# Routing weights spread over partitions by DMAs and multiplied in by GpSimd, in place of TensorE's spreading products

## The reference

```python
xV = einsum('btd,kdr->btkr', Q_side, V)          # r = 64 per expert
cum_yW = cumsum(einsum('btd,kdr->btkr', K_side, W), axis=1)
weights = softmax(gelu(Q_side @ w1.T + b1) @ w2.T + b2 + expert_bias)
out = einsum('btkr,kdr->btd', xV * cum_yW * weights[..., None], U)
out = (out + weights @ b) / n_valid              # n_valid: 1, 2, 3, ...
```

## Time and profile before

| what | value |
|---|---|
| median of 3 runs | 1653.61 us (1653.0 to 1655.18) |
| profiled execution | 1654.62 us, span 1652.9 us |
| mean granted TensorE clock | 0.996 |
| busy: PE / DVE / ACT / POOL | 1563.5 / 937.7 / 684.4 / 284.2 us |
| DMA | 116.48 MB, 38.5% of 16 engines' span |

### The profile page before, as it was taken

How to read it: one execution, slowest core, us unless ns; L and a number is a source line. 1 busy time by engine, 2 the same in 40 slices (tenths; PEclk the granted TensorE clock), 3 DMA queues, 4 the chain that set the end, 5 groups by cost and what they waited for, 6 DMA issues and landing times.

```text
span 1652.9 us, 36914 instructions
## 1 busy us (share of the span) xinstructions
PE 1563.5 (95%) x15489; PEld 1112.8 (67%) x15489; DVE 937.7 (57%) x2048; ACT 684.4 (41%) x1224; POOL 284.2 (17%) x346
## 2 busy tenths in 40 slices
PE   5899999999999999999999999999999999999997
PEld 4576675767757676676757767576675767667674
DVE  6665672737537484564837567274763748447461
ACT  3426245261543517243362523626254351634425
POOL 2011121211112111121201212021111201112111
PEclk9999999999999999999999999999999999999999
DMA  8514417072350906218071350806326080530800
GB/s 207 63 31 88 80 34 123 10 117 51 76 89 4 151 15 104 61 38 130 4 122 45 77 91 21 125 21 106 62 64 100 4 139 27 96 69 23 132 4 14
DMA packets 128186, 116.48 MB, mean 70 GB/s; under 512 B 19251, under 2 KB 127668, under 8 KB 127972
## 3 DMA queue, kind: packets, MB, share of 16 engines
q1 hardware_dynamic: 128020, 114.12, 38.5%
HBM read 73.43 MB, written 34.34 MB: 65 GB/s over the span
## 4 chain that ended last, share of the span: by engine, by line
PE 76%; DVE 14%; ACT 5%; issue 4%; POOL 1%; DMA 0%; DVEq 0%; ACTq 0%; POOLq 0%
PE PS L587 33%; PE PS L714 8%; DVE block_peak L1204 4%; PE PS L793 3%; PE PS L825 3%; PE PS L732 3%; PE PS L856 3%; PE PS L766 3%; PE PS L807 3%; PE PS L772 3%; DVE prod L1273 2%; PE PS L726 2%; DVE prod L1276 2%; ACT HE L1029 2%; PE PS L746 2%
## 5 line engine op out<-in xcount | busy, mean ns | idle before, releaser
L1446 POOL TENSOR_TENSOR PL<-prod,PH 128x512 fp32r<-128x512 f32 x128 | 164.5, 1285 | 792.7 <-ACT PH L1003 792.7
L1003 ACT ACTIVATE PH<-prod 128x512 fp32r<-128x512 f32 x128 | 80.8, 631 | 428.8 <-DVE prod L1276 428.8
L587 PE MATMUL PS<-XH,WH 128*128 128x512 f32 x512 | 220.4, 430 | 4.5 <-DVE XL L1145 1.9
L587 PE MATMUL PS<-XH,WL 128*128 128x512 f32 x512 | 203.6, 398 | 0.0
L587 PE MATMUL PS<-XL,WH 128*128 128x512 f32 x512 | 203.2, 397 | 0.0
L1204 DVE TENSOR_REDUCE block_peak<-PS 128x4 f32<-128x512 f32 x288 | 186.9, 684 | 4.2 <-PE PS L746 4.2
L993 ACT ACTIVATE prod<-PS 128x512 f32<-128x512 f32 x128 | 76.3, 596 | 231.3 <-PE PS L587 220.3
L1029 ACT ACTIVATE HE<-PS 128x512 f32<-128x512 f32 (+1 forms) x320 | 159.7, 552 | 26.1 <-PE PS L807 23.5
L1197 DVE TENSOR_REDUCE peak<-PS 128x4 f32<-128x512 f32 x192 | 125.6, 685 | 41.0 <-PE PS L732 41.0
L1273 DVE TENSOR_TENSOR prod<-PS,prod 128x512 f32<-128x512 f32 x128 | 88.1, 689 | 104.6 <-PE PS L701 104.6
L714 PE MATMUL PS<-UH,PH 128*128 128x256 f32 x512 | 139.5, 306 | 0.0
(11 more groups left out here) (195 smaller groups left out, 3154.8 us busy)
## 6 DMA issues: line engine op xcount, KB each, us to landing
parts_d<-area SPq DMA_DIRECT2D x32, 768.0 KB, 5.1
area<-parts_d SPq DMA_DIRECT2D x128, 192.0 KB, 12.4
area<-parts_d SPq DMA_DIRECT2D x32, 576.0 KB, 12.5
tok<-in_L_attn_x_dram SPq DMA_DIRECT2D x16, 512.0 KB, 6.5
xt<-in_L_attn_x_dram SPq DMA_DIRECT2D x16, 512.0 KB, 3.9
out_dram<-xt SPq DMA_DIRECT2D x16, 512.0 KB, 3.7
area<-parts_d SPq DMA_DIRECT2D x96, 64.0 KB, 5.9
Vs<-Va SPq DMA_DIRECT2D x24, 204.0 KB, 7.6
```

The costliest lines, as they stand in the source:

```text
L587: ins = e.matmul(ps, a, b, start=first and k == 0, stop=last and k == n - 1, skip_group_check=True)
L1003: e.activation(PH[:, h, :], prod[:, j % 3, :], ACT.Copy).then_inc(phi)
L1446: e.tensor_tensor(PL[:, j % 2, :], prod[:, j % 3, :], PH[:, j % 2, :].bitcast(F32), ALU.subtract).then_inc(plo)
```

## The change

TensorE's `product` matmul, the matrix `spread` with its memset and its three selects, bank 4's use by `product` and the semaphore `w_ps` are removed. In `gate_parts` VectorE also turns the float32 gates (in 32x32 blocks) into `weights_t`; SP writes that to DRAM (`weights_d`) in four DMAs, waits for them, and for each block j reads two rows of it back, each repeated over 64 partitions, into one of three 128x512 buffers `wide` (two of them are `rest`). GpSimd multiplies `prod` by it in place, in the new stage `weigh`, which stands in the list right behind the x stage of the block. VectorE's `product` keeps the multiplication by bank 3 only and waits for `weigh`. Blocks 0 to 2 are read back in the stage `gate_parts` itself; block j + 3 after block j's `weigh`. ScalarE's copy to `WT` no longer waits for `w_ps`, and the running sum of the next chunk waits for the last `weigh` stages, since it overwrites `rest`.

```diff
@@ the list of stages
-                order.append([(add_x, ch, j + 1, part) for part in range(2)])
+                order.append([(add_x, ch, j + 1, part) for part in range(2)] + [(add_weigh, ch, j + 1)])
...
     def add_product(ch, j):
-        add("product", ch, j, uses=["bank4"])
+        add("product", ch, j)
+
+    def add_weigh(ch, j):
+        add("weigh", ch, j)
+        if j + WIDE < 2 * KB:
+            add_wide(ch, j + WIDE)
+
+    def add_wide(ch, j):
+        add("wide", ch, j, uses=[f"wide{j % WIDE}"])
+
+    def add_gate_parts(ch):
+        add("gate_parts", ch)
+        for j in range(WIDE):
+            add_wide(ch, j)
...
         add_cout(ch, 0)
         if nxt:
+            add_weigh(ch + 1, 0)
             run([(add_x, ch + 1, 1, part) for part in range(2)])
+            add_weigh(ch + 1, 1)
         for k in range(DB):
             add_on("cparts", ch, k, uses=[score_use()])
         if nxt:
             run([(add_x, ch + 1, 2, part) for part in range(2)])
+            add_weigh(ch + 1, 2)
         add_finish(ch)
@@ buffers
-        spread = sb("spread", [KSTK, 2 * KB, P], BF16)
+        weights_t = sb("weights_t", [P, T * 32])
+        wide = [rest[:, 0, :], rest[:, 1, :], sb("wide2", [P, C])[:, :]]
+        weights_d = nc.dram_tensor("weights_d", (2 * KE, C), F32, kind="Internal").ap()
@@ TensorE
-                elif kind == "product":
-                    ch, j = key
-                    q.wait_ge(bank_read[7], use("bank7", "weight_rows", ch))
-                    take(4, *stage)
-                    e.matmul(psum(4), spread[:, j, :], WT[:, :], start=True, stop=True).then_inc(w_ps)
@@ VectorE, turn
+                        q.wait_ge(weighed, nth("weigh", ch - 1, 6 + k))
@@ VectorE, gate_parts
+                    q.wait_ge(weights_out, 16 * 4 * ch)
+                    e.transpose(weights_t[:, :].rearrange("p (t w k) -> p t w k", t=T, w=2),
+                                gate[:, 2:4].rearrange("p w t k -> p t w k")).then_inc(weights_turned)
+                    q.wait_ge(weights_turned, ch + 1)
@@ VectorE, product
-                    q.wait_ge(bank_read[2], use("bank2", "x", ch, j, 0))
-                    q.wait_ge(w_ps, nth(*stage))
-                    e.tensor_tensor(prod[:, r, :], psum(4), prod[:, r, :], ALU.mult).then_inc(bank_read[4])
-                    q.wait_ge(bank_read[4], use("bank4", *stage))
+                    q.wait_ge(weighed, nth("weigh", ch, j))
                     q.wait_ge(c_ps, nth(*stage))
                     e.tensor_tensor(prod[:, r, :], psum(3), prod[:, r, :], ALU.mult).then_inc(bank_read[3])
@@ GpSimd
-                    for n, first in enumerate((0, 3 * HD, 5 * HD)):
-                        view = spread[:, :, :].rearrange("r j (a m) -> r (j a) m", a=2)
-                        select(view, [[-1, 4 * KB], [0, R]], -first, 1, ALU.not_equal, 1.0, after=8 + n if n else 0)
...
+                elif kind == "weigh":
+                    ch, j = key
+                    q.wait_ge(bank_read[2], use("bank2", "x", ch, j, 0))
+                    q.wait_ge(wide_in[j % WIDE], 16 * use(f"wide{j % WIDE}", "wide", ch, j))
+                    e.tensor_tensor(prod[:, j % 3, :], prod[:, j % 3, :], wide[j % WIDE], ALU.mult).then_inc(weighed)
@@ SP
+                elif kind == "gate_parts":
+                    ch, = key
+                    q.wait_ge(weights_turned, ch + 1)
+                    for i in range(WIDE):
+                        q.wait_ge(wide_in[i], 16 * (use(f"wide{i}", "wide", ch, i) - 1))
+                    for g in range(4):
+                        e.dma_start(weights_d.rearrange("k (t g r) -> g k t r", t=T, g=4)[g],
+                                    weights_t[32 * g:32 * g + 2 * KE, :].rearrange("k (t r) -> k t r", t=T)).then_inc(weights_out, 16)
+                elif kind == "wide":
+                    ch, j = key
+                    q.wait_ge(weights_out, 16 * 4 * (ch + 1))
+                    if j >= WIDE:
+                        q.wait_ge(weighed, nth("weigh", ch, j - WIDE))
+                    elif j == 2:
+                        q.wait_ge(weighed, nth("weigh", ch - 1, 5))
+                    else:
+                        q.wait_ge(part3, nth("parts", ch, 0, DB - 1))
+                        q.wait_ge(clo, DB * (ch + 1))
...
+                    e.dma_start(wide[j % WIDE], weights_d[2 * j:2 * j + 2, :].unsqueeze(1).to_broadcast([2, R, C])).then_inc(wide_in[j % WIDE], 16)
```

More of the change, by code:

```diff
@@ L87, in mixer_layer @@
     HE_SLOTS = 6
+    WIDE = 3
     assert DB == 2 and NC == 2 and KR == 512 and NG == 4 and NL % 4 == 0 and C // WINDOW == 8
@@ L316, in mixer_layer @@
         add_on("fold_u", n, uses=[fold_use()])
-    add("gate_parts", 0)
+    add_gate_parts(0)
     for part in range(2):
         add_x(0, 0, part)
+    add_weigh(0, 0)
     for part in range(2):
@@ L359, in mixer_layer @@
             order = order[1:]
-            side = [[(add_gates, ch + 1)], [(add, "gate_parts", ch + 1)]] + [[]] * (2 * (ch % NC))
+            side = [[(add_gates, ch + 1)], [(add_gate_parts, ch + 1)]] + [[]] * (2 * (ch % NC))
             side += [[(add_values, ch + 1, 0)], [(add_values, ch + 1, 1)]]
@@ L511, in mixer_layer @@
         logits_ps, gate_max, gate_exp, gate_split, gate_turned = (sem(n) for n in ("logits_ps", "gate_max", "gate_exp", "gate_split", "gate_turned"))
-        x_ps, c_ps, w_ps, phi, plo = (sem(n) for n in ("x_ps", "c_ps", "w_ps", "phi", "plo"))
+        x_ps, c_ps, phi, plo = (sem(n) for n in ("x_ps", "c_ps", "phi", "plo"))
+        weights_turned, weights_out, weighed = (sem(n) for n in ("weights_turned", "weights_out", "weighed"))
+        wide_in = [sem(f"wide{i}_in") for i in range(WIDE)]
         lpeaks_ps, gpeaks_ps, lscores_ps, gscores_ps, ctx_turned, ctx_hi, out_ps = (
@@ L530, in mixer_layer @@
         N_RAW = [11, 5, 8, 5, 1]
-        N_SELECT = 14
+        N_SELECT = 11
         products = [stage for stage in plan.stages if stage[0] in ("alpha", "join", "fold", "bias_row", "fold_u")]
@@ L979, in scalar_program @@
                         q.wait_ge(bias_in, 16 * 15)
-                    q.wait_ge(w_ps, 2 * KB * ch)
                     e.activation(WT[:, :], PS[0:KSTK, 7, :].bitcast(BF16)[:, 0:C], ACT.Copy).then_inc(bank_read[7])
@@ L1105, in vector_program @@
                         e.memset(view, 0.0).then_inc(blank)
-                    for view in (ident, ident_b, peak_mask_l, peak_mask_g, spread, mask_l):
+                    for view in (ident, ident_b, peak_mask_l, peak_mask_g, mask_l):
                         e.memset(view[:], 0.0).then_inc(cleared)
@@ L1399, in gpsimd_program @@
                 if kind == "boot":
-                    q.wait_ge(cleared, 6)
+                    q.wait_ge(cleared, 5)
                     for n, view in enumerate((ident[:, :], ident_b[:, :])):
@@ L1408, in gpsimd_program @@
                     select(peak_mask_l[0:64, 1, :], [[1, P]], -WINDOW, 0, after=7)
-                    for n, first in enumerate((0, 3 * HD, 5 * HD)):
-                        view = spread[:, :, :].rearrange("r j (a m) -> r (j a) m", a=2)
-                        select(view, [[-1, 4 * KB], [0, R]], -first, 1, ALU.not_equal, 1.0, after=8 + n if n else 0)
                     select(mask_l[:, :], [[-1, WINDOW]], 0, 1)
-                    select(mask_l[:, :], [[1, WINDOW]], WINDOW, -1, after=12)
+                    select(mask_l[:, :], [[1, WINDOW]], WINDOW, -1, after=9)
                     e.iota(positions[:, :], pattern=[[P, ST]], base=1, channel_multiplier=1).then_inc(selected)
@@ L1440, in gpsimd_program @@
                                         channel_multiplier=-1).then_inc(global_masked)
+                elif kind == "weigh":
[3 more added lines that the diff above has]
+                    e.tensor_tensor(prod[:, j % 3, :], prod[:, j % 3, :], wide[j % WIDE], ALU.mult).then_inc(weighed)
                 elif kind == "product":
                     ch, j = key
-                    q.wait_step()
                     q.wait_ge(phi, nth(*stage))
@@ L1555, in sync_program @@
                     e.dma_start(QS[G16:KSTK, lo:lo + n, :], peak_d[which].rearrange("(a h) t -> a h t", h=n)).then_inc(peak_in[which], 16)
+                elif kind == "gate_parts":
[16 more added lines that the diff above has]
+                        q.wait_ge(clo, DB * (ch + 1))
+                        if ch == 0:
+                            q.wait_ge(bias_in, 16 * 15)
+                    e.dma_start(wide[j % WIDE], weights_d[2 * j:2 * j + 2, :].unsqueeze(1).to_broadcast([2, R, C])).then_inc(wide_in[j % WIDE], 16)
                 elif kind == "finish":
```

## The result

The changed kernel takes 1834.34 us (median of 4 runs, 1827.58 to 1836.08) against 1654.39 us for the kernel before on the same chip (4 runs, 1653.0 to 1655.66): a ratio of 1.1078, 95% interval 1.1055 to 1.1101. It is slower by 180 us, where 1634.5 had been forecast. The profiled execution has a span of 1833.5 us.

What follows compares the result with a forecast made beforehand. TensorE was taken as the bound, busy 1563.5 of 1652.9 us. Terms: 29.4 + 12 + 3.3 + 1.7 - 14.2 - 6.4 - 6.7 = 19.1 us off 1654.6, less 1.0: 1634.5 us, range 1605 to 1652.

Steps and rivals of the forecast that it cites:

- the price of one read: At chunk starts: reading one 256 KB block of weights back from DRAM was estimated at 2.8 us from issue to landing.
- GpSimd's step "at nothing": In GpSimd's queue: 128 added multiplications of 1285 ns, 164 us more work, were costed at nothing, being one block ahead.
- the readback becomes the bound: Rival at chunk starts: each read lands in 7.6 us, 9 places x 4.8 = 43 us lost, 1677.5 us; chance 0.10.
- None is late by this: Behind the waiting SP: Vs copies, global stacks (moved some 9 us) and the store were all claimed to be in time.
- In even chunks ... a way of some 6: hidden: Even chunk starts: the first product comes 11 us after the Vs copies' issue, the weights need some 6, no wait.
- The clock: TensorE at chunk starts: three odd chunks and the first lose 1.7 us each at half speed, -6.7 us, bounds 0 and -15.
- The wait of an odd chunk: Start of each of eight odd chunks: TensorE idles 1.8 us more, -14.2 us in all, bounds nothing to 6.6 us each.
- The off-loading itself: Savings: TensorE's spreading products 29.4 us, its waits for VectorE 12 us, first normalization without the spreading mask's selects 1.7 us.
- all hidden: Rival at chunk starts: small writes land before the stacks, no chunk waits, 50 us gained, 1603.5 us; chance 0.22.
- the masks: First normalization: without GpSimd's three selects for the spreading mask, the chain to the first transposes is 1.7 us shorter.
- The port rival: Expert stages: small VectorE steps wait for GpSimd at the shared SBUF port, 27 us of VectorE's time, 1661.5 us; chance 0.05.
- no change: Rival: TensorE's savings become idle time at chunk starts, clock -8 more, no VectorE relief (-12), about 1653 us; chance 0.07.

## Why the prediction was wrong

**The step that failed is the price of one read, "which lands in 2.8 us".** It was scaled by bytes from a load of 512 KB to all partitions, and that load has another shape: 128 partitions outermost. The read of the change has 2 outermost and was there after 7.8 us, and the second and third, which the sum did not charge at all, came 5.7 and 7.5 us behind each other. With 64 partitions outermost one half of the block, 128 KB, takes 2.9 us and both halves 4.2, so even then the price was low for a whole block. The answer on the first DMA of the reads by expert, issued at 378.35 (tiles, queue, count, KB, us from issue to landing):

```profile
rest<-weights_d SPq DMA_DIRECT2D x1, 128.0 KB, 2.9
```

**GpSimd's step "at nothing" failed with it.** The prediction had "only the earlier block's subtraction" behind a multiplication in GpSimd's queue, needed a block later. At a chunk's start the multiplications of blocks 1 and 2 stand ahead of block 0's subtraction, and once the reads came one behind the other this order cost the larger of the two waits, 89.4 us in 16 places. With the reads by expert that wait is not among TensorE's waits at all, so the order costs only where a read is late.

**The rival "the readback becomes the bound" was the right one and too cheap.** Its 7.6 us a read happens to be the first read's time, but its reasons (one row for 64 partitions, small pieces) were not the cause, as the reads by expert keep both. It counted one read in nine places. What came was three reads in sixteen places, with GpSimd's order making block 0 wait for block 2. It thus gave 1677.5 for what measures 1834.

**The reads also hold up SP.** "None is late by this" was said of what stands behind SP. SP's timeline after the reads were issued, and the same copy with the reads by expert:

```profile
408.49 2.89 SPq L1598 DMA_DIRECT2D wide<-weights_d  x1
411.48 5.15 SPq L1556 DMA_DIRECT2D Vs<-Va  x1
```

```profile
382.60 0.66 SPq L1556 DMA_DIRECT2D Vs<-Va  x1
```

The third read takes 2.89 us to issue and the first copy into Vs 5.15 us, where a copy took 0.62 before and this one 0.66 with the reads by expert. That the time went there is not shown: the chain passes through the reads.

**"In even chunks ... a way of some 6: hidden" failed for the same reason.** The first product of the even chunks is not late, but block 0's mixing products are: the wait on L731 comes 16 times, not 8.

**The clock was mis-sized by the largest factor.** I let four stretches of half clock cost 6.7 us, 15 at most. The changed kernel's trace has 27 such stretches. Against the kernel without reading back, TensorE's busy time for the same 15361 matmuls is 1607.2 against 1530.2, so 77 us of the 224 between the two spans are slower matmuls; the other 147 are idle, nearly all of it in the two waits above (89.4 + 61.2, less the 10.9 that the other kernel has too). Even with the reads by expert, 22.6 of 44.5 us are slower matmuls (busy 1552.8). It had been sized by rows at two lengths of idle time, 0.64 and 2.55 us.

**The wait of an odd chunk would have been too small even with a good read.** I took 1.8 us for each. With the reads by expert the first product comes 3.4 us later in relation to L than without reading back (6.1 against 2.7). The two halves of a read cost 4.2 us from the first issue and not 2.9, and the writes land 0.8 and not 0.4 behind the stacks; that is 1.7 us, about the whole of the difference.

**What was right.** The small writes land just behind the stacks, in spite of the gates that are ready early; issuing them from a second queue did not change that. GpSimd's multiplication takes its 1285 ns (rows that answer to the earlier trace rows: its subtraction, then the new multiplication, by form):

```profile
L1466 POOL TENSOR_TENSOR PL<-prod,PH 128x512 fp32r<-128x512 f32 x128 | 163.2, 1280 | 159.3 <-ACT PH L1019 159.1
...
L1461 POOL TENSOR_TENSOR prod<-prod,rest 128x512 f32<-128x512 f32 x96 | 123.2, 1284 | 528.4 <-DMA rest<-weights_d 393.9 <-ACT prod L1009 134.4
```

The off-loading itself is worth what the sum said: 29.4 + 12 + 1.7 (with 3.3 and 3.7 in the case of all hidden, 50 us) against 43 us without reading back, which still has 10.9 us of wait in its first chunk, so some 54 without that. VectorE's waits gave 10.9 of the 12. Later reads, three blocks ahead, are hidden. With reads by expert the first chunk's product ended at 96.5, and 96.05 was forecast, in part by luck: the residual load was issued 1.1 us earlier than taken (77.60), and the read took 3.6 us from its issue and not 2.9. And the masks: the steps of the first normalization that took 1.02 and 1.05 us are short now that GpSimd's selects are gone:

```profile
6.94 0.17 DVE L1139 TENSOR_SCALAR var<-mv 128x4 f32<-128x4 f32 x1
7.15 0.17 DVE L1141 TENSOR_SCALAR var<-var 128x4 int32<-128x4 int32 x1
7.35 0.17 DVE L1143 TENSOR_SCALAR var<-var 128x4 int32<-128x4 int32 x1
```

**The port rival came true for VectorE and not for TensorE.** Two of the 4-column steps of the norms, over the whole run, before and without reading back (L1123 there is L1139 here, L1125 is L1141; count, busy us, mean ns):

```profile
L1123 DVE TENSOR_SCALAR var<-mv 128x4 f32<-128x4 f32 x16 | 3.6, 223 | 0.5
...
L1125 DVE TENSOR_SCALAR var<-var 128x4 int32<-128x4 int32 x16 | 2.6, 160 | 0.0
```

```profile
L1141 DVE TENSOR_SCALAR var<-var 128x4 int32<-128x4 int32 x16 | 7.5, 468 | 0.0
...
L1139 DVE TENSOR_SCALAR var<-mv 128x4 f32<-128x4 f32 x16 | 7.5, 466 | 0.5
```

With a third kind of step (239 to 383 ns, 48 times) that is 15.7 us more of VectorE's time, where the rival had 27, and each of the long steps ends within 0.05 us of the end of a GpSimd instruction that began before it. So one of the prediction's own signs of being wrong, growing 4-column steps, is there. But GpSimd works as long there as in the change (443.9 us) and the gain of 43 us is there all the same: TensorE did not feel it.

One sum of the rivals was off by itself: 19.1 less 8 and 12 is 0.9 us slower than before, so "no change" adds up to 1654.5 and not to 1653.

## What to carry to other kernels

Price a transfer by a row of the same shape and not by its bytes: the outermost dimension of the DMA decides how many engines carry it, and a read of 256 KB with 2 outermost was there after 7.8 us where two of 128 KB with 64 outermost were there in 4.2. When a value goes through DRAM with a deadline, ask what the 16 engines are carrying at that moment, whichever queue issues it, and what stands behind the waiting instruction in each in-order queue. Where only the first use after a boundary is late, keep the old way for that one and send the rest by the new: with the reads by expert and one to three of eight blocks spread by TensorE, the kernel is 2.2 to 2.4% faster than before, where the change as it stood was 10.8% slower.

## What was not expected of the hardware

A short idle stretch at a boundary cost as much again in slow matmuls: with the reads by expert the first product came 3.4 us later at each of eight boundaries, and the trace has 57 us more at half clock than without reading back, 44 of them in the stretches that begin at these boundaries. Of the 44.5 us between the two spans, 22.6 are slower matmuls. And an issue on SP is not always some 0.6 us: behind reads that only two engines carry, single issues took 2.89 to 5.15 us, and the same copy 0.66 us behind the reads by expert.
